# Issuing later adjacency tiles from ScalarE, and regrouping key forms and the opening, in a masked attention layer

## The reference

```python
h = jnp.maximum(_layernorm(x, axis=-1), 0.0)
lQ, lK, lV = mx @ Wlq, h @ Wlk, h @ Wlv + blv
gQ, gK, gV = mx @ Wgq, x_bar @ Wgk, x_bar @ Wgv + bgv      # x_bar: mean of h over rows
es, eV = mx @ Wes, mx @ Wev + bev
local_scores = jnp.where(adj, lQ @ lK.T * scale, -1e9)
global_scores = gQ @ gK.T * scale
max_score = max(rowmax(local_scores), global_scores, es)
le, ge, ee = exp(local_scores - max_score), exp(global_scores - max_score), exp(es - max_score)
denom = sum(le) + ge + ee
res = le / denom @ lV + ge / denom * gV + ee / denom * eV
return x + jnp.maximum(res, mx)
```

## Time and profile before

| | |
|---|---|
| median of 3 runs | 742.03 us (741.88 to 742.55) |
| the profiled execution | 740.42 us |
| its span, first to last instruction | 738.7 us |
| PE busy | 720.9 us, 98% of the span |
| DVE busy | 587.1 us, 79% |
| ACT busy | 528.5 us, 72% |
| POOL busy | 445.4 us, 60% |
| adjacency loads on SP | 64 of 256 KB, 3.4 us from issue to landing |
| transposes of probabilities on SP | 120, 4.5 us from issue to landing |

### The profile page before, as it was taken

The page is one execution under the profiler, slowest core; times in us unless marked ns, Lnnn a source line. Parts: engine busy times, 40 slices in busy tenths (PEclk is TensorE's granted clock), DMA queues, the critical chain, the costliest instruction groups (busy, mean ns, idle before and its releaser), DMA issues. The chain is left out here.

```text
span 738.7 us, 14671 instructions
## 1 busy us (share of the span) xinstructions
PE 720.9 (98%) x5232; PEld 509.6 (69%) x5232; DVE 587.1 (79%) x1352; ACT 528.5 (72%) x699; POOL 445.4 (60%) x314
## 2 busy tenths in 40 slices
PE   8989999989999999999999999999999999999998
PEld 6657566756676777676776767676766677666787
DVE  5887787988788778887888888887888788877645
ACT  5864876676867777778767777787768777777690
POOL 3769689969456554655456555655466455644583
PEclk9999999999999999999999999999999999999999
DMA  7693486787888799888978698788979798788797
GB/s 241 154 181 88 94 176 146 159 166 152 159 177 178 150 188 155 179 167 163 185 154 180 137 209 161 161 170 166 187 146 181 138 210 149 169 179 170 128 194 152
DMA packets 360874, 121.89 MB, mean 165 GB/s; under 512 B 320992, under 2 KB 360800, under 8 KB 360800
## 3 DMA queue, kind: packets, MB, share of 16 engines
q1 hardware_dynamic: 360256, 120.42, 80.6%
q10 hardware_dynamic: 544, 0.52, 0.2%
HBM read 36.57 MB, written 4.19 MB: 55 GB/s over the span
## 5 line engine op out<-in xcount | busy, mean ns | idle before, releaser
L607 POOL TENSOR_TENSOR p_base<-s,p_base 128x1024 f16<-128x1024 f32 x108 | 233.2, 2160 | 221.9 <-ACT p_base L817 221.8
L1090 PE MATMUL ps_u<-v_rows,pT_base 128*128 128x256 f16 x968 | 263.9, 273 | 0.0
L1092 PE MATMUL ps_u<-v_rows,pT_base 128*128 128x256 f16 x968 | 263.9, 273 | 0.0
L1094 PE MATMUL ps_u<-v_rows,pT_base 128*128 128x256 f16 x968 | 263.9, 273 | 0.0
L782 ACT ACTIVATE bias<-adj,big 128x1024 f32<-128x1024 uint8 x127 | 156.2, 1236 | 136.5 <-DVE bmax L1438 129.0
L795 ACT ACTIVATE s<-s,negm,invc 128x1024 f32<-128x1024 f32 x128 | 157.0, 1226 | 6.4 <-DVE negm L1494 6.4
L817 ACT ACTIVATE p_base<-s 128x1024 f16<-128x1024 f32 x122 | 129.0, 1057 | 19.8 <-DMA pT_base<-p_base 16.4
L1090 PEld LDWEIGHTS ps_u<-v_rows,pT_base 128*128 128x128 f16 x968 | 94.7, 98 | 52.2
L1092 PEld LDWEIGHTS ps_u<-v_rows,pT_base 128*128 128x128 f16 x968 | 94.7, 98 | 52.1
L1438 DVE CUSTOM_DVE_ANT_0 s<-ps_x,bias 128x512 f32<-128x512 f32 x128 | 87.1, 685 | 34.4 <-PE ps_x L991 32.4
L1094 PEld LDWEIGHTS ps_u<-v_rows,pT_base 128*128 128x128 f16 x968 | 94.7, 98 | 11.0
(11 more groups left out here) (238 smaller groups left out, 1299.3 us busy)
## 6 DMA issues: line engine op xcount, KB each, us to landing
adj<-adj SPq DMA_DIRECT2D x64, 256.0 KB, 3.4
s<-x SPq DMA_DIRECT2D x7, 512.0 KB, 4.5
f32q<-mx SPq DMA_DIRECT2D x14, 256.0 KB, 3.7
xm<-x SPq DMA_DIRECT2D x14, 256.0 KB, 3.5
xm<-mx SPq DMA_DIRECT2D x14, 256.0 KB, 4.0
out<-t_sb SPq DMA_DIRECT2D x14, 256.0 KB, 3.4
pT_base<-p_base SPq DMA_TRANSPOSE x120, 4.5
mxT_f<-mxT SPq DMA_DIRECT2D x4, 256.0 KB, 4.3
```

The lines of the kernel that those rows point to most:

```text
L607: nc.gpsimd.tensor_tensor(p_rows(u)[:, 1], s32[:, p % NS, u % 2], p_rows(u)[:, 0], ALU.subtract).then_inc(s_plo, 1)
L1090: nc.tensor.matmul(acc, turn[:, 0, j], v_rows[:, kc, 0:D], start=opens, stop=False, skip_group_check=True)
L1092: nc.tensor.matmul(acc, turn[:, 0, j], v_rows[:, kc, D:2 * D], start=False, stop=False, skip_group_check=True)
L1094: done = nc.tensor.matmul(acc, turn[:, 1, j], v_rows[:, kc, 0:D], start=False, stop=end, skip_group_check=True)
```

## The change

The adjacency tiles of periods 5 to 63 are issued by ACT on its own queue; tiles 0 to 4 stay on SP. In ACT's loop the load of period p + 2 stands behind the first unit's exponential and high half. In the opening, x block 7 is loaded one block later; tiles 2 and 3 go from blocks 3 and 5 to blocks 4 and 5, tile 2 ahead of x block 7; the global weights, `Wgv`, `Wes` go one block later, and `Wev` behind tile 4. On POOL the sums and halves of `keys_t3` become one function; group 0's sums go from ahead of the query's low half to behind it, and groups 2 and 3 each go one period earlier. In ACT's list, block 5's value halves go ahead of its mask. On TensorE, `project(1)` goes behind the turned half and query of tile 1.

```diff
@@ -256,7 +256,7 @@
         V_OUT_AT = {4: (0, 1, 2), 5: (3, 4), 6: (5, 6, 7), 7: (8,)}
         BIAS_AT = {4: (2, 3), 5: (4,), 6: (5,), 7: (6,)}
         OUT_AT = {5: (2,), 6: (3,), 7: (4,)}
-        X_AT = {1: (4, 5), 2: (6,), 3: (7,)}
+        X_AT = {1: (4, 5), 2: (6,), 4: (7,)}
         Q1_AT = 7
         HALVES = 3
         TP = 2
@@ -443,28 +443,26 @@
                     transpose_h(g)
                 if g == 1:
                     load_adj(1)
+                if g in (4, 5):
+                    load_adj(g - 2)
                 for k in X_AT.get(g, ()):
                     load_x(k)
-                if g == 4:
+                if g == 5:
                     for dst, src in ((wgq_t, WgqT), (wgk_t, WgkT)):
                         sp.dma_start(dst, cols(src)).then_inc(s_wg, 16)
-                if g == 5:
+                if g == 6:
                     sp.dma_start(wgv_sb, cols(Wgv)).then_inc(s_wgv, 16)
                     with nc.allow_non_contiguous_dma(reason="a column of 256 words"):
                         sp.dma_start(mge[:, :, D + 1:D + 2], cols(Wes)).then_inc(s_wgv, 16)
-                if g in (3, 5):
-                    load_adj(g // 2 + 1)
                 if g == 6:
-                    sp.dma_start(wev_sb[:, :, :], cols(Wev)).then_inc(s_wev, 16)
                     for dst, src in ((blv_b, blv), (bev_b, bev), (bgv_b, bgv)):
                         sp.dma_start(dst[:, :], src.partition_broadcast(P)).then_inc(s_bc, 16)
             transpose_q(1)
             load_adj(4)
+            sp.dma_start(wev_sb[:, :, :], cols(Wev)).then_inc(s_wev, 16)
             load_mxT_q(2)
 
             for p in range(4, NPER + LAG_E + 1):
-                if p + 1 < NPER:
-                    load_adj(p + 1)
                 if p == 4:
                     transpose_p(0)
                 if p % NG == 0 and QH <= (p + 4) // NG < NP:
@@ -562,7 +560,7 @@
                 forms(twv[:, 0], twv[:, 0], plain(g, 1, 0, 1), ALU.add)
                 split(tw[:, 0], mixed(g, 2, 0), mixed(g, 2, 1), s_t4)
 
-            def keys_t3_sums(g):
+            def keys_t3(g):
                 if g == 0:
                     pool.wait_ge(s_t4, NG)
                 else:
@@ -572,8 +570,6 @@
                 forms(twv[:, 0], plain(g, 1, 1, 0), plain(g, 1, 1, 1), ALU.add)
                 forms(twv[:, 0], twv[:, 0], plain(g, 0, 1, 0), ALU.subtract)
                 forms(twv[:, 0], twv[:, 0], plain(g, 0, 1, 1), ALU.subtract)
-
-            def keys_t3_halves(g):
                 split(twv[:, 0], plain(g, 0, 1, 0), plain(g, 0, 1, 1), s_t3)
 
             def q_sums(n):
@@ -636,16 +632,12 @@
                 n = (p + 2) // NG
                 if p % NG == 2 and 2 <= n < NP and NG * n >= PC:
                     q_sums(n)
-                if p == PC - 2:
-                    keys_t3_sums(0)
                 if live:
                     p_low(u)
                 if p % NG == 2 and 2 <= n < NP:
                     q_low(n)
                 if p in (PC - 2, PC - 1):
-                    if p == PC - 1:
-                        keys_t3_sums(1)
-                    keys_t3_halves(p - PC + 2)
+                    keys_t3(p - PC + 2)
                 if p == NPER + 2:
                     finish(NP - 3)
                 if live:
@@ -660,9 +652,8 @@
                     keys_t2(p // 2 - 1)
                 if p in (5, 7, 9):
                     keys_t4((p - 3) // 2)
-                if p in (PC, PC + 1):
-                    keys_t3_sums(p - PC + 2)
-                    keys_t3_halves(p - PC + 2)
+                if p in (PC - 1, PC):
+                    keys_t3(p - PC + 3)
             pool.wait_ge(s_xm_end, 32)
             nc.gpsimd.tensor_tensor(edge_rows[:, 1], edge_rows[:, 1], edge_rows[:, 0], ALU.add).then_inc(s_rest_end, 1)
             pool.wait_ge(s_e_end, 2)
@@ -815,6 +806,12 @@
                 elif u >= 2:
                     act.wait_ge(*turned(u - 2))
                 nc.scalar.activation(p_rows(u)[:, 0], s32[:, p % NS, t], ACT.Copy).then_inc(s_phi, 1)
+
+            def load_adj(p):
+
+                act.wait_ge(s_bias, 2 * (p - 1))
+                n, g = p // NG, p % NG
+                act.dma_start(adj8[:, p % 2], adj_pairs[n][:, :, g * GROUP:(g + 1) * GROUP]).then_inc(s_adj[p % 2], 16)
 
 
             act.dma_start(wk_t, WlkT.rearrange("(c p) d -> p c d", p=P)).then_inc(s_wqk, 16)
@@ -853,22 +850,26 @@
                         v_high(n)
                 if 4 < g < NB - 1:
                     h_deviation(g + 1)
+                if g == 5:
+                    for n in V_OUT_AT[g]:
+                        v_high(n)
                 for u in BIAS_AT.get(g, ()):
                     mask_bias(u)
                 if g == 4:
                     h_deviation(g + 1)
-                    continue
                 if g == Q1_AT:
                     q_scale(1)
                     q_high(1)
-                for n in V_OUT_AT[g]:
-                    v_high(n)
+                if g >= 6:
+                    for n in V_OUT_AT[g]:
+                        v_high(n)
             mask_bias(7)
             for n in V_AT[NB - 1]:
                 v_high(n)
             mask_bias(8)
             for n in V_AT[NB]:
                 v_high(n)
+            load_adj(5)
             for p in range(4, NPER + LAG_E):
                 if p < NPER:
                     mask_bias(2 * p + 1)
@@ -888,6 +889,8 @@
                     p_high(u)
                     if u % (2 * NG) == 0:
                         side_exp((p - LAG_E) // NG)
+                if p + 2 < NPER:
+                    load_adj(p + 2)
                 if p % NG == 2 and 2 <= n < NP:
                     q_high(n)
                 if p == 7:
@@ -1182,9 +1185,9 @@
             pe.wait_ge(s_const, 4)
             turn_half(0, 0)
             turn_q(0)
-            project(1, D)
             turn_half(0, 1)
             turn_q(1)
+            project(1, D)
             for b in range(1, NB):
                 for t in range(2):
                     classic((b - 1) // 2, t, (b - 1) % 2)
```

## The result

The changed kernel took 746.53 us (median of 7 runs, 743.71 to 747.90), the kernel before 741.88 (7 runs beside it). The ratio is 1.0053, 95% interval 1.0036 to 1.0070: slower, where 739.2 was forecast. The profiled execution took 747.90, with a span of 746.2 us against 738.7, so it is the slowest of the seven; what is read from it is held against the runs further on. (A ratio here is formed on its own and is not the quotient of the medians: by the ratio the loss is 3.9 us, by the medians 4.65.)

A forecast was written before the change was run, and what follows sets the result against it. TensorE bounds the dense main loop; four long early waits, 8.3 us, were within reach. Gains 0.75 + 0.85 + 0.3 + 0.9 + 0 = 2.8 us give 737.6 in the profile's terms, 739.2 as median; range 736.2 to 742.8.

The forecast's parts named there:

- Part 1: TensorE's opening order: `project(1)` later lets the first score product start at 14.9, not 15.66; 0.75 us gained.
- Part 2: Opening loads: the 2.39 us wait at keys 4 goes, a new one comes at keys 6; 1.6 us gained with Part 1.
- Part 3: `keys_t3` on POOL: 0.3 of the 3.07 us wait at 151.01 gained, and 0.9 of the 1.76 at 185.22.
- to spare in the period of `p_low(14)`: `p_low(14)` comes about 2 us later; the DVE output waiting for it has 1 us spare, the key product behind 0.5.
- Part 4: Main loop, 59 adjacency loads issued by ACT: idle time and waits cover the issues; sum 0, at best 1.3 us gained.
- (c): Query's low half period: ACT's issue beyond about 1 us delays halves, DVE and bank; at 1.5 us, 6 lost: 745; chance 0.13.
- (d): Main loop: descriptor-generator lock makes ACT's issue last 3.59 us like SP's transpose; 47 us lost, 789; chance 0.04.
- (a): Keys 6 in time and the 3.07 us wait largely gone, since DVE really waits for a transpose: 736; chance 0.17.
- (b): Opening gains nothing, with keys 6 landing at 52.6 or DVE waiting for x block 7; 0.9 us left: 741.1; chance 0.20.
- what I named beforehand as showing me wrong: ACT's issues over 1 us; ACT waiting less for DVE while TensorE waits more at low query halves; idle before group 12 gone.

The follow-up runs named there:

- parts 1 and 2 alone: The kernel before with only the new order of the opening (loads on SP, ACT's list, `project(1)` later): 740.90 us against 741.51, ratio 0.9991.
- all but part 4: The changed kernel with adjacency loads of periods 5 to 63 back on SP, opening and key forms as changed: 740.53 us, ratio 0.9991 to the kernel before.
- part 4 alone: The kernel before with only the adjacency loads of periods 5 to 63 issued by ACT on its own queue: 746.61 us against 741.51, ratio 1.0073.
- quarter on ACT: The kernel before with only the 14 adjacency loads of periods with p mod 4 = 3 issued by ACT: 745.08 us against 741.33, ratio 1.0048.
- p mod 4 = 0 on ACT: The kernel before with only the 14 adjacency loads of periods with p mod 4 = 0 issued by ACT: 743.01 us against 741.70, ratio 1.0017.

## Why the prediction was wrong, by its steps

**Part 1** held: the first score product started at 14.71, forecast 14.9, without a wait.

**Part 2** was right in its places. Keys 4: 2.39 us of wait became 0.53, forecast none. Their transpose was issued at 32.70 (forecast 33.0) with no plain load just ahead, and still took 6.1 us to land, not 4.3: without the two loads ahead it is 1.5 us less than the 7.5, where 3.2 were forecast. Keys 6: a new wait of 2.65, forecast about 2 (2.55 with parts 1 and 2 alone, 0.23 in the profile of all but part 4, where keys 3 were 1.51 late in its place). The first `ps_v` product of keys 7 began at 60.25 before, at 59.17 with parts 1 and 2 alone and at 58.73 with all but part 4: 1.1 and 1.5 us ahead, where 1.6 were forecast. In the changed kernel's own profile keys 7 were late too (0.73) and it began at 60.28. Parts 1 and 2 give 0.6 us by the medians, and not that 1.1 to 1.5. The clock's falls below may have taken the rest; that is not shown.

**Part 3** gave nothing, where 1.2 was forecast. The rows of all but part 4:

```profile
149.84 0.38 PE L985 MATMUL ps_x<-hT,qT 128*128 128x512 f16 x1 [3.42 <-DVE bmax L1434]
...
162.83 0.39 PE L985 MATMUL ps_v<-hW,qT 128*128 128x512 f16 x1 [0.41 <-DVE bmax L1434]
...
170.39 0.39 PE L985 MATMUL ps_x<-hT,qT 128*128 128x512 f16 x1 [0.22 <-DVE bmax L1434]
...
183.94 0.39 PE L985 MATMUL ps_v<-hW,qT 128*128 128x512 f16 x1 [0.97 <-DVE bmax L1434]
```

1.76 became 0.97, as worked out, but what I called to spare in the period of `p_low(14)` was not: 0.41 and 0.22 are new, and the long wait grew from 3.07 to 3.42. In sum 5.02 against 4.98, with this one of the kernel before:

```profile
173.51 0.39 PE L989 MATMUL ps_v<-hW,qT 128*128 128x512 f16 x1 [0.15 <-DVE bmax L1438]
```

**Part 4 is the step that failed**: "Sum of part 4: 0". Of a moved DMA I priced the issue, 0.57 us (it is 0.37), and the time at which its tile is wanted. I did not price the 256 KB it moves, and what they move beside. On one queue the load was kept behind the transposes by order alone. "the transposes start up to 0.6 us sooner, TensorE does not wait for one of them" was true of the kernel before and was taken for slack: the earlier trace rows had ACT waiting 0.93 us for a transpose at 433.72, with TensorE waiting 0.20 us at 438.01. I read the 0.93 as cover for ACT's issue; it was the sign that transposes were already late for ACT. It was not even the transpose that the harm came to, the one behind the query's, but one issued a period earlier behind two loads of rows, 7.0 us before it landed. Both are below. For the second, the one behind the query's, ACT waited 0.24 us here and 1.49 us at 360.30:

```profile
426.59 3.41 SPq L370 DMA_TRANSPOSE pT_base<-p_base  x1
...
438.17 2.89 SPq L370 DMA_TRANSPOSE pT_base<-p_base  x1
...
443.07 1.06 ACT L817 ACTIVATE p_base<-s 128x1024 f16<-128x1024 f32 x1 [0.24 <-DMA pT_base<-p_base]
```

With part 4 alone ACT's waits for the transposes behind the query's grew from 5.8 to 20.8 us (after 180 us), and those for the ones behind the loads of rows from 4.1 to 8.0. With the quarter on ACT they are 17.5 and 4.0: those fourteen loads touch the first kind alone.

**The rivals.** (c) named the right chain (ACT's second high half, POOL's low half, DVE, the bank,'s 438.01) and nearly the right time, 745, with the wrong cause: ACT's issue time, which costs nothing that can be told. That its time came out is luck. (d), the locked generator, is refuted: 59 issues took 373 to 440 ns beside transposes whose issue took SP 3.3 us. The Trainium skill (Perfetto Trace Analysis, DMA Instruction — HWDGE) would have ACT wait for the lock there; no row shows it. Nor did SP's issues suffer: a transpose of `mx` took 1.24 us to issue before, and 1.24 us with an issue of ACT beside it in 12 of 13 cases (p mod 4 = 0 on ACT, medians). (a) and (b) spoke only of the parts that came out near zero. Of what I named beforehand as showing me wrong, one came true: TensorE waits more in the periods of low query halves and the ones after them (p mod 4 = 2 and 3), while ACT waits for DVE less.

## What to carry over

A load moved to another engine's queue is not only an issue moved: it leaves the order that kept its bytes behind the urgent transfers. Before moving one, list which transfers on the old queue someone waits for, and place the load so that it is issued when none of them is under way. A wait of 0.2 us on the bounding engine in an otherwise dense loop was the sign here that the chain behind it had no slack left.

## What the runs showed of the hardware

- The transpose of probabilities that stands behind a query's transpose and a load of `mx` took 4.9 us to land (mean of 11), 5.7 with 128 KB and 5.9 with 256 KB beside it on the other queue. The same 256 KB behind it on its own queue: 4.9.
- An issue of a plain copy of 256 KB held ACT for 0.37 us, SP for 0.57 (median).
- TensorE's granted clock fell to 0.50 (1.2 GHz) for 3.4 us, in three cases 6.8, in three places, in some profiles and not in others. At 42 to 46 us, behind the 2.4 us of idle time ahead of keys 4: in 3 of 11 profiles with the old opening and in none of 6 with the new one, where that idle time is shorter. At 64 to 74 us, behind some 3 us with short matmuls (128x1 and 128x2): in 1 of 11 and in 4 of 6. At 148 to 160, around the 3 us of idle time ahead of period 12: in 3 of 11 and 3 of 6. In the changed kernel it cost 1.7 us at each of the last two (64:68 at 0.90 and 68:72 at 0.68; 152:154 at 0.63 and 154:156 at 0.52). That the new opening causes the fall at 64 is likely by the count, but was not tried. One profile can't price a gain of 1 to 2 us in the opening.
